# Four small edits at the joints of a fused transformer layer: last penalties, weight slots, layer norm's gain, and a loop of two trips

## The reference, cut to what matters

```
emb = silu(sin_emb(timestep)) @ W_ada + b_ada; scale, shift = split(emb)
x = ln(src) * (1 + scale) + shift
q, k, v = x @ Wq + bq, x @ Wk + bk, x @ Wv + bv        (by heads)
scores = q k' / sqrt(32) + attention_bias, masked where src_mask
ctx = softmax(scores) v
x = x + (ctx @ Wo + bo)
h = ln(x) * g2 + beta2
out = x + gelu2(h @ W1 + b1) @ W2 + b2, then pairs of columns rotated by theta and phi
```

## Time and profile before

| | us |
|---|---|
| median of 3 runs | 3461.2 (3459.51 to 3461.22) |
| the profiled execution | 3459.6 |
| its span, first to last instruction | 3457.9 |
| PE busy | 3401.9 (98%) |
| DVE busy | 2473.3 (72%) |
| ACT busy | 1874.1 (54%) |
| POOL busy | 2118.7 (61%) |
| mean granted TensorE clock | 0.994 of full |

### The profile page before, as it was taken

One profiled execution on the slowest core, in us unless ns is written; L12 is line 12 of the kernel. 1 busy time (PEld: TensorE's weight loads), 2 busy tenths in 40 slices (PEclk: granted clock), 3 DMA queues, 4 the chain that ended last, 5 costly groups with the idle time before them and its releaser, 6 DMA issues. The chain is left out here.

```text
span 3457.9 us, 60344 instructions
## 1 busy us (share of the span) xinstructions
PE 3401.9 (98%) x18230; PEld 1931.1 (56%) x18230; DVE 2473.3 (72%) x4130; ACT 1874.1 (54%) x2515; POOL 2118.7 (61%) x674
## 2 busy tenths in 40 slices
PE   8999799999999999999999999999899999999998
PEld 3444466666666666666666666666444444444443
DVE  5665599999999999999999999999434334343331
ACT  3222388888888888888888888888111111111010
POOL 0000499999899999899999999998303212221200
PEclk9999899999999999999999999999999999999999
DMA  8999999999999999999999999999823123132000
GB/s 296 342 342 330 380 364 346 346 351 348 397 347 350 350 342 352 399 347 342 353 348 348 392 352 350 349 344 320 234 45 85 43 49 79 42 66 62 12 12 13
DMA packets 243407, 913.81 MB, mean 264 GB/s; under 512 B 27568, under 2 KB 44464, under 8 KB 166064
## 3 DMA queue, kind: packets, MB, share of 16 engines
q1 hardware_dynamic: 177920, 810.38, 65.5%
q10 hardware_dynamic: 62896, 94.65, 7.9%
q0 software_dynamic: 2560, 8.39, 0.7%
HBM read 770.46 MB, written 142.87 MB: 264 GB/s over the span
## 5 line engine op out<-in xcount | busy, mean ns | idle before, releaser
L675 POOL TENSOR_TENSOR ring<-ring,penb 128x1856 f32<-128x1856 f32 x511 | 1898.4, 3760 | 129.3 <-DMA ring<-in_fside_Bx16xSxS 87.3
L784 ACT ACTIVATE ring<-ring,low 128x2048 f32<-128x2048 f32 x512 | 1029.1, 2010 | 299.6 <-DVE low L752 299.5
L866 PEld LDWEIGHTS b_T<-ident,ring 128*128 128x128 f32 x8192 | 890.3, 141 | 430.5 <-DVE probT L736 428.2
L866 PE MATMUL b_T<-ident,ring 128*128 128x128 f32 x8192 | 1091.7, 276 | 3.3 <-DVE probT L736 3.3
L752 DVE CUSTOM_DVE_ANT_0 ring<-scores,ring 128x1024 f32<-128x1024 f32 x512 | 627.1, 1225 | 173.4 <-PE scores L832 157.0
L736 DVE COPY probT<-b_T 128x512 f32<-128x512 f32 x1024 | 702.9, 687 | 4.2 <-PE b_T L866 4.1
L752 DVE CUSTOM_DVE_ANT_0 ring<-scores,ring,low_part 128x1024 f32<-128x1024 f32 x512 | 653.0, 1275 | 1.2 <-issue 0.5
L832 PE MATMUL scores<-keys,queries 128*128 (+1 forms) x2048 | 621.7, 425 | 15.3 <-ACT ring L784 11.9
L889 PE MATMUL bank_ctx<-probT,values 128*32 128x512 f32 x4096 | 545.3, 605 | 0.0
L796 ACT COPY probT<-b_T 128x512 f32<-128x512 f32 x1024 | 538.7, 576 | 2.8 <-PE b_T L866 2.7
L1218 ACT ACTIVATE keys_again<-scores,b_scaled 128x512 f32<-128x512 f32 x128 | 88.0, 687 | 732.5 <-PE scores L1442 732.5
(11 more groups left out here) (134 smaller groups left out, 2068.5 us busy)
## 6 DMA issues: line engine op xcount, KB each, us to landing
ring<-in_fside_Bx16xSxS SPq DMA_DIRECT2D x512, 1024.0 KB, 7.5
keys<-k_rows SPq DMA_DIRECT2D x64, 1024.0 KB, 8.4
queries<-q_rows SPq DMA_DIRECT2D x128, 256.0 KB, 8.0
values<-v_heads ACTq DMA_DIRECT2D x128, 256.0 KB, 6.4
ctx_scratch<-ctxp ACTq DMA_DIRECT2D x128, 256.0 KB, 6.3
penb<-ctx_scratch SPq DMA_DIRECT2D x120, 256.0 KB, 10.3
k_rows<-part_hi SPq DMA_DIRECT2D x64, 256.0 KB, 3.1
k_rows<-part_lo SPq DMA_DIRECT2D x64, 256.0 KB, 3.1
```

The lines of the kernel that those rows point to most:

```text
L675: nc.gpsimd.tensor_tensor(ring[:, j, 0:POOL_MASKED], ring[:, j, 0:POOL_MASKED], penb[:, j, 0:POOL_MASKED], ALU.add).then_inc(masked, 1)
L784: nc.scalar.activation(ring[:, k, :], ring[:, k, :], ACT.Exp, bias=low[:, k:k + 1], scale=-1.0, accum_out=column(sums_all, trip, k)).then_ ...
L866: last = nc.tensor.transpose(turn_bank(slot, n)[:, c * P:(c + 1) * P], ring[:, slot, at:at + P], ident[:])
```

## The change

It has four parts.

1. Last penalties. The penalties of the last block go to slots 5 and 6 of `ring` (`last_pen`) instead of `penb`. ScalarE waits for the last store of `xm` and for the last turning before it writes them. SP stores them at g = 7 of the last block, between the stores of groups 6 and 7, not at the end. In the attention's first trip SP waits for that store at j = 5, not at 4, and the wait for `xm`'s store goes.
2. Weight slots. W1 takes slots 2 to 5 of `ring` and W2 the slots 6, 7, 0 and 1. The four pieces of W1 are loaded in order after the turns of tiles 2 to 5 of the last trip, b2 is loaded after them, then two pieces of W2 after the turns of tiles 6 and 7, and the last two after the context has left slots 0 and 1. TensorE's first projection waits for each piece of the context just ahead of its matmul, no longer for all four ahead of the first.
3. g2 and beta2 are loaded as columns, one value a partition, and ScalarE applies them in the copy of the turned rows (an Identity activation with scale and bias). VectorE's multiplications and additions with them go, and so do their loads as rows.
4. The attention's loop over trips 1 to 63 becomes a loop of 31 passes with two trips each, and trip 63 is written out.

```diff
+        last_pen = streams.ring[:, 5:7, :].bitcast(BF16).rearrange("p a (t n) -> p (a t) n", n=S)
...
-                             pen.rearrange("p t n -> p (t n)")).then_inc(pen_stored, 16)
+                             (last_pen if last_tile(u) else pen).rearrange("p t n -> p (t n)")).then_inc(pen_stored, 16)
...
+                    if g == 7 and last_tile(u):
+                        store_pen(u)
                     sp.wait_ge(staged, u * 2 * DB + g + 1)
...
             sp.wait_ge(ada_used, 5)
+            sp.wait_ge(pen_stored, 16 + (NU - 1) * 16)
             for j in range(Streams.EARLY, PREFETCHED):
                 attention_tile(j)
-            store_pen(NU - 1)
...
+                if t == 0 and last_tile(u):
+                    act.wait_ge(xm_stored, NU * 16)
+                    act.wait_ge(xt_psum, NU * DB + 4)
...
-            if j == PREFETCHED:
+            if j == 5:
                 sp.wait_ge(stored.pen, 16 + NU * 16)
-                sp.wait_ge(stored.xm, NU * 16)
...
-        with eng.Fori(1, TRIPS) as it:
-            for j in range(R):
-                step(it, j)
+        with eng.Fori(0, TRIPS // 2 - 1) as pair:
+            for k in range(2):
+                for j in range(R):
+                    step(pair * 2 + 1 + k, j)
+        for j in range(R):
+            step(TRIPS - 1, j)
...
-    w1 = ring[:, 0:4, :]
-    w2 = places(ring, 4, 4).rearrange("p (f n) -> p f n", n=D)
+    w1 = ring[:, 2:6, :]
+    w2 = [places(ring, slot, 1).rearrange("p (f n) -> p f n", n=D) for slot in (6, 7, 0, 1)]
...
-        for c in (2, 3):
-            after_turns(c)
+        for c in range(4):
+            after_turns(2 + c)
             load_w1(c)
         after_scores(7)
         sp.dma_start(b2_all, row(b2)).then_inc(vec_in, 16)
-        sp.dma_start(g2_all, row(g2)).then_inc(vec_in, 16)
-        sp.dma_start(beta2_all, row(beta2)).then_inc(vec_in, 16)
-        for c in range(4):
-            after_turns(4 + c)
+        for c in range(2):
+            after_turns(6 + c)
             load_w2(c)
         for c in range(2):
             sp.wait_ge(ctxT_ready, 3 + c)
-            load_w1(c)
+            load_w2(2 + c)
...
+        def scaled_rows(to, turned, c):
+
+            nc.scalar.activation(to, turned, ACT.Identity, scale=g2_col[:, c:c + 1], bias=beta2_col[:, c:c + 1]).then_inc(hT_ready, 1)
+
+        act.wait_ge(vec_in, 64)
         for c in range(DB):
             act.wait_ge(h_turned, c + 1)
-            nc.scalar.copy(hT[:, 0, c, :], acc[c]).then_inc(hT_ready, 1)
+            scaled_rows(hT[:, 0, c, :], acc[c], c)
...
-                link(nc.vector.tensor_scalar(hn[:, t, :], x2[:, 0, t, :], mean_var[:, t, 0:1], rstd[:, t:t + 1], ALU.subtract, ALU.mult))
-                link(nc.vector.tensor_tensor(hn[:, t, :], hn[:, t, :], g2_all, ALU.mult))
-                nc.vector.tensor_tensor(hn[:, t, :], hn[:, t, :], beta2_all, ALU.add).then_inc(first_hn, 1)
+                nc.vector.tensor_scalar(hn[:, t, :], x2[:, 0, t, :], mean_var[:, t, 0:1], rstd[:, t:t + 1], ALU.subtract, ALU.mult).then_inc(first_hn, 1)
...
         def first_wo(t):
             for c in range(DB):
+                if t == 0:
+                    pe.wait_ge(ctxT_ready, c + 1)
```

More of the change, by code:

```diff
@@ L340, in penalty @@
                     act.wait_ge(pen_stored, u * 16 + 16)
-                nc.scalar.activation(pen[:, t, :], mask_in[:, t, :], ACT.Copy, scale=MASKED).then_inc(pen_ready, 1)
+                if t == 0 and last_tile(u):
+                    act.wait_ge(xm_stored, NU * 16)
+                    act.wait_ge(xt_psum, NU * DB + 4)
+                nc.scalar.activation((last_pen if last_tile(u) else pen)[:, t, :], mask_in[:, t, :], ACT.Copy, scale=MASKED).then_inc(pen_ready, 1)
             act.dma_start(w_ada, W_ada.rearrange("(c p) n -> p c n", p=P)).then_inc(w_ada_in, 16)
@@ L938, in phase_c @@
     per_row = places(penb, 6, 1).rearrange("p (a n) -> p a n", n=TOK)
-    g2_all, beta2_all = places(penb, 7, 1)[:, 0:D], places(penb, 7, 1)[:, D:2 * D]
     bo_all, b2_all = (left.queries[:, i, :] for i in range(2))
@@ L957, in phase_c @@
     b1_col = sb("b1_col", [P, FB])
+    g2_col = sb("g2_col", [P, DB])
+    beta2_col = sb("beta2_col", [P, DB])
     b1_scaled = sb("b1_scaled", [P, FB])
@@ L1074, in load_w2 @@
         def load_w2(c):
-            sp.dma_start(w2[:, 4 * c:4 * c + 4, :], W2.rearrange("(c p) n -> p c n", p=P)[:, 4 * c:4 * c + 4, :]).then_inc(w2_in, 16)
-        sp.dma_start(b1_col[:], b1.rearrange("(c p) -> p c", p=P), allow_slow_non_contiguous=True).then_inc(vec_in, 16)
+            sp.dma_start(w2[c], W2.rearrange("(c p) n -> p c n", p=P)[:, 4 * c:4 * c + 4, :]).then_inc(w2_in, 16)
+        for to, v in ((b1_col, b1), (g2_col, g2), (beta2_col, beta2)):
+            sp.dma_start(to[:], v.rearrange("(c p) -> p c", p=P), allow_slow_non_contiguous=True).then_inc(vec_in, 16)
         sp.wait_ge(left.scored, left.SCORED0 + LAST * CH)
@@ L1209, in front @@
                 act.wait_ge(h_turned, v * DB + c + 1)
-                nc.scalar.copy(hT[:, bass.ds(v % 2, 1), c, :].rearrange("p o n -> p (o n)"), fore[c % 2]).then_inc(hT_ready, 1)
+                scaled_rows(hT[:, bass.ds(v % 2, 1), c, :].rearrange("p o n -> p (o n)"), fore[c % 2], c)
         def ffn(u, f):
@@ L1238, in vector @@
     def vector(dve):
-        LINKS = 6
+        LINKS = 4
         def first_front():
@@ L1322, in front @@
                     last = nc.vector.tensor_scalar(hn[:, t, :], x2_v[:, t, :], mean_var[:, t, 0:1], rstd[:, t:t + 1], ALU.subtract, ALU.mult)
-                link(last, 4)
-            if f == 11:
-                for t in range(QT):
-                    last = nc.vector.tensor_tensor(hn[:, t, :], hn[:, t, :], g2_all, ALU.mult)
-                link(last, 5)
-                for t in range(QT):
-                    last = nc.vector.tensor_tensor(hn[:, t, :], hn[:, t, :], beta2_all, ALU.add)
                 last.then_inc(hn_ready, 1)
@@ L1452, in ffn @@
                 for t in range(QT):
-                    last = nc.tensor.matmul(acc[t], hidden[:, k % 4, t * P:(t + 1) * P], w2[:, k, :], start=(k == 0), stop=(k == FB - 1))
+                    last = nc.tensor.matmul(acc[t], hidden[:, k % 4, t * P:(t + 1) * P], w2[k // 4][:, k % 4, :], start=(k == 0), stop=(k == FB - 1))
                 last.then_inc(down_done, 1)
@@ L1458, in ffn @@
                     for k in range(FB - LAST_BY_TILE, FB):
-                        last = nc.tensor.matmul(acc[t], hidden[:, k % 4, t * P:(t + 1) * P], w2[:, k, :], start=False, stop=(k == FB - 1))
+                        last = nc.tensor.matmul(acc[t], hidden[:, k % 4, t * P:(t + 1) * P], w2[k // 4][:, k % 4, :], start=False, stop=(k == FB - 1))
                     last.then_inc(down_done, 1)
@@ L1463, in tensor @@
         pe.wait_ge(wo_in, 16)
-        pe.wait_ge(ctxT_ready, DB)
         first_wo(0)
```

## The result

| | before | after |
|---|---|---|
| median of 18 runs each | 3461.2 (3459.25 to 3466.15) | 3467.5 (3464.09 to 3470.85) |
| profiled execution, its span | 3459.6, 3457.9 | 3467.1, 3465.4 |
| trip 1 opens | 422.59 | 430.62 |
| trip 63 opens | 2383.27 | 2386.25 |
| first feed-forward block opens | 2455.82 | 2461.20 |

The ratio is 1.0016, 95% interval [1.0009, 1.0022]: slower by 6.3 us where 4.9 us less were forecast. In the profiled executions it is 7.5 us: 8.0 lost before trip 1 opens, 5.1 gained between trip 1 and trip 63, 2.4 lost between trip 63 and the first block, 2.1 in the first block. Every later block takes 125.4 us in both.

What follows compares the result with a forecast made beforehand. TensorE's queue of work was taken to bound most of the span. Loop -3.2, first passage -0.9 and feed-forward start -0.8 sum to -4.9 us, giving 3456.3, said as 3456; range 3449 to 3466.

Steps and rivals of the forecast that it cites:

- the first passage: Projection to attention, about 360 to 430 us: GpSimd's second tile of trip 1 lands at about 423.2, 0.9 us gained.
- passes when about a third have gone: Values' store on ScalarE's queue: the next issue passes after about a third of 2048 packets, by 388 us instead of 392.7.
- Rival (4): First passage: the values' store starved by SP's transfers, ScalarE held until near 406; 8 us lost, 3465 to 3470, chance 0.08.
- The loop: Attention's 63 trips: key-slot register instructions fall out, 0.05 us a trip, 3.2 us gained; halved branches worth nothing on TensorE.
- Rows, W1, W2 and columns: Attention to feed-forward: shorter VectorE rows against later b2 and longer copies; feed-forward starts at 2455.0, 0.8 us earlier.
- b2's row: Before feed-forward: b2, issued behind all of W1, lands at about 2439.6, so VectorE's chain starts at 2440.3 instead of 2436.08.
- their landing moves away from the start: Feed-forward start: W1's pieces come before W2's, so W2's landing moves away from the start; no cost priced.
- Passage 2: Passage from attention to feed-forward, 2415 to 2456 us, where feed-forward was forecast to start 0.8 us earlier.

Runs made afterwards that it cites:

- e8: Kernel after, with SP waiting for the values' store before it issues tile 4 of trip 0: 3461.1 us, ratio 1.0002.
- e4: Kernel after with the later wait: first copies wait only for key and query stores, ScalarE waits for the values' store at tile 7; 3459.1 us, ratio 0.9989.
- e1: Kernel before with the last penalties' edit (part 1) alone: 3468.3 us, ratio 1.0017.
- e2: Kernel before with the loop of two trips a pass (part 4) alone: 3459.9 us, ratio 0.9991.
- e10: Kernel after with the key slot kept as an expression of the loop counter, worked out in registers each trip: 3471.3 us, ratio 1.0025.
- e9: Kernel after with four trips a pass in every engine's loop and the last three trips written out: 3565.2 us, ratio 1.0303.
- e3: Kernel before with the new weight slots and g2 and beta2 as columns (parts 2 and 3) alone: 3462.7 us, ratio 1.0000.
- e6: Kernel after with e4's edit and b2 on a semaphore of its own, waited for at the first residual: 3461.0 us, ratio 1.0000.
- e13: Kernel before with parts 1 and 4 and e4's edit, weights and columns as before: 3459.7 us, ratio 0.9992.
- e12: e6 with only half of each piece of W1 and W2 loaded, a probe that leaves out needed data: 3454.1 us, ratio 0.9973.
- e5: Kernel after with e4's edit and the three column loads (b1, g2, beta2) issued at trip 16: 3458.0 us, ratio 0.9987.

## Why the prediction was wrong

**The step that failed** is in the first passage: "The exponential starts some 4 us earlier. None of it reaches the end, because the landing above decides." I followed ScalarE to the end of its DMA issues and to the exponential, and let GpSimd's landing decide. The next kind of work on ScalarE, its first copy of a turned tile, waits for all of phase A's stores, the values' too (`all_groups`, at tile 2). In the kernel before that wait cost nothing, since the store landed at 397.2 and the copy came due at 399.93, so no view of waits showed it. I had the cause in hand: packets of q1 and q10 go one for one, and q10's are small. I used it to price the *issue* and not the *landing* of the same store. With SP no longer waiting at tile 4, q1 stays filled from 378 to 408 and the store lands 11.4 us later (e8 shows that it is this, e4 that it is this wait, e1 that part 1 does it alone). Term: -0.9 forecast, +8.0 measured. The landing of GpSimd's tile, which the term was made of, was nearly right (423.2 forecast, 424.74 measured), but it wasn't what ended last.

The forecast of ScalarE's issue was wrong too: free at 388, said the rule "passes when about a third have gone"; measured 393.8 (393.6 before). When an issue passes in a shared queue I can't say from these runs.

**Rival (4) gave the right number by a neighbouring path.** It had the store starved by SP's transfers right, and trip 1 opening "near 431 instead of 422.6: 8 us lost"; measured 430.6. It laid the blame on ScalarE's issue, held until 406; in fact the issue passed at 393.8 and the wait for the landing came after it. That its number came out is in part luck. I gave it 0.08.

**The loop.** Mechanism right, size small: -3.2 forecast, -4.6 measured over trips 2 to 62. Another 0.5 of the 5.1 us lies in trip 1, which took 32.0 us and now 31.54; that isn't the loop's, since trip 1 takes 31.98 in e2, with the new loop alone, and 31.58 in e1, with the old loop and the late start. The four register instructions of the key slot go altogether, where I had taken half of their price, and the opening tile is 3.95. Halving the branches is worth nothing that shows (e10), and a body of two trips needs no code fetch (the kernel after), where one of four does (e9). The Trainium skill's "Advanced Engine Details and Errata", section ISA Cache, has only 2 cache lines of 256 instructions; the trace disagrees: with a body of some 1,000 instructions, for which five blocks of 16 KB are fetched from 421.7 to 488.7 us, none is fetched for TensorE from there until 2397.2. Where the runs show an end is between that body and one of twice the size (e9).

**Rows, W1, W2 and columns.** -0.8 forecast, +2.4 measured before the first block and +2.1 in it. Of the sum, the rows were right (2.79 for 2.9). The copies were not: the activation with scale and bias takes 0.777 us, not 0.687, so four of them cost 0.8 and not 0.4. (No table load came with it: there are 21 in both kernels.) The small loads were not either (Wo lands 3.6 us later against the opening of trip 63, where I took 1.3), and b2's row followed: 2446.5 against the forecast 2439.6, of which 3.0 is the later trip 63 and 2.3 the small loads; 1.6 is left. But e3, e6 and e13 show that this was the wrong account to keep. Opening the first block sooner gives nothing, since block 1's context isn't ready; I had said "their landing moves away from the start" of the weights and priced the rest at nothing without asking what is queued behind W2. What counts is the volume of transfers in front of the last context part (e12), which parts 2 and 3 hardly change. Passage 2 also takes back some of the loop's gain: in the profiles all of it (e2: 5.0 gained, 4.9 given back before the block opens, 1.1 in it), by the medians some 2 us of 5. Of the 4.5 us that the kernel after loses behind trip 63, e13 and e2, which lose 5.5 and 6.0 without parts 2 and 3, say that none is due to these parts; what it is due to stays open.

**Sum.** -3.2 - 0.9 - 0.8 was forecast; -5.1 + 8.0 + 4.5 is what the profiles show; the medians differ by 6.3.

**A version that beats both.** The kernel after with the later wait: 0.9989 [0.9980, 0.9998]; with trip 1 instead of 63 written out 0.9988 [0.9979, 0.9997]; with the columns at trip 16, 0.9987 [0.9978, 0.9996]. That is 0.1% below the kernel before, with intervals that just leave out no change, and by the ratios 9 to 10 us below the kernel after. The three can't be told apart.

## What to carry to other kernels

When an edit lets more transfers out sooner, list every wait in the program for a transfer that is still under way at that moment, also those that now cost nothing, and ask when each lands beside the new traffic. A wait that no row shows is not a wait that isn't there; it is one whose slack you must read off (landing 397.2, due 399.9: 2.7 us). And where the DMA engines are full, as in passage 2, price an edit by the bytes in front of the last transfer that someone waits for, not by the wait that it removes.

## What the runs showed of the hardware that was not expected

- The last of the values' stores, in packets of 512 bytes, landed 19.5 us after its issue where no bias tile was issued meanwhile (377.80 to 397.34, e8) and 30.6 us after it where three were (378.03 to 408.64, the kernel after).
- Loading 3,072 values of four bytes, one a packet, cost some 3 us even in the middle of the attention: for 10 us the DMA engines moved 154 GB/s instead of 343, and TensorE lost it two trips later (e5).
- TensorE kept a loop of five 16 KB blocks without a fetch for 1,900 us; with twice the body it fetched about ten blocks a pass and lost 6.6 us a pass, part of it to a lower granted clock behind the wait (0.67 from 560 to 570, e9).
- Four register instructions of 0.05 us in front of a weight load, once a trip, made the trip 0.074 us longer (31.617 for 31.543, e10).
